# Attention of the experts: the input products of the recurrence are taken out of PSUM by ScalarE instead of VectorE

## The reference

```
h = _ln(relu(x @ ew1 + eb1) @ ew2 + eb2, eg, ebeta)
q, k, v = split(h @ aiw + aib)                       # 16 heads of 16
attn = softmax(einsum('bhqd,bhkd->bhqk', q, k) * SCALE)
h = einsum('bhqk,bhkd->bhqd', attn, v) @ aow + aob
# recurrence, forward and backward in time:
zg = xt @ Wi + h @ Wh + b                            # i, f, g, o gates, 4 x 256
```

## Time and profile before

| what | value |
|---|---|
| median of 3 runs | 6249.12 us (6246.4 to 6255.38) |
| the profiled execution, its own time | 6250.81 us |
| span of its trace | 6248.8 us |
| attention of the experts (all blocks) | about 790 to 2465 us |
| recurrence | about 2472 to 5860 us |
| mean granted TensorE clock | 0.964 of full speed |

### The profile page before, as it was taken

The page is one execution under the profiler, slowest core; times in us unless marked ns, Lnnn a source line. Parts: engine busy times, 40 slices in busy tenths (PEclk is TensorE's granted clock), DMA queues, the critical chain, the costliest instruction groups (busy, mean ns, idle before and its releaser), DMA issues. The chain is left out here.

```text
span 6248.8 us, 161662 instructions
## 1 busy us (share of the span) xinstructions
PE 5595.9 (90%) x59552; PEld 2263.0 (36%) x59552; DVE 4774.4 (76%) x14157; ACT 2351.6 (38%) x8487; POOL 1726.4 (28%) x8205
## 2 busy tenths in 40 slices
PE   7978788889899897999999999999999999998895
PEld 4545423233333232333333333333333333333443
DVE  4545676667576766999999999999999999994224
ACT  2334354355454444333333333333333333333332
POOL 0000000000000000555555555555555555552000
PEclk9989989999999998999999999999999999999997
DMA  0003443343432444011101110111101111012110
GB/s 12 0 24 129 127 80 78 95 73 74 94 74 64 93 89 139 19 34 20 34 14 34 20 34 24 24 34 20 34 14 34 33 21 34 14 20 69 35 68 10
DMA packets 378689, 303.02 MB, mean 48 GB/s; under 512 B 146073, under 2 KB 358681, under 8 KB 373562
## 3 DMA queue, kind: packets, MB, share of 16 engines
q1 hardware_dynamic: 378510, 301.15, 20.3%
HBM read 182.09 MB, written 120.59 MB: 48 GB/s over the span
## 5 line engine op out<-in xcount | busy, mean ns | idle before, releaser
L1300 PE MATMUL bank<-lparts,lstate 128*32 128x512 bf16 x49152 | 3006.1, 383 | 214.8 <-POOL lstate L1387 96.5
L1300 PEld LDWEIGHTS bank<-lparts,lstate 128*32 128x32 bf16 x49152 | 1133.0, 97 | 2088.2 <-POOL lstate L1387 1183.1
L1312 DVE STREAM_TRANSPOSE ltz<-bank 128x512 f32<-128x512 f32 x2048 | 1464.9, 715 | 129.8 <-PE bank L1300 51.4
L1357 ACT ACTIVATE lgate<-lz 128x48 f32<-128x48 f32 x2048 | 497.9, 243 | 2078.5 <-DVE lz L1318 2077.1
L1318 DVE TENSOR_REDUCE lz<-ltz 128x64 f32<-128x256 f32 x2048 | 1270.6, 620 | 0.0
L1051 DVE TENSOR_REDUCE bnegmax<-bank 128x1 f32<-128x512 f32 x1024 | 649.8, 680 | 251.2 <-PE bank L981 250.3
L1384 POOL TENSOR_TENSOR lstate<-lstate 128x16 f32<-128x16 f32 x2048 | 439.4, 215 | 1324.4 <-DVE lstate L1332 1250.4
L1270 POOL MEMSET lstate<- 128x256 f32 x1 | 0.3, 312 | 2471.4 <-POOLq L61 2471.4
L1096 ACT ACTIVATE wh<-bank 128x512 f32<-128x512 f32 x1024 | 554.4, 598 | 295.3 <-PE bank L1003 288.3
L1394 POOL COPY ltz<-wh 128x64 f32<-128x64 f32 x2048 | 593.6, 290 | 0.0
L883 PE MATMUL bank<-xT,bw 128*128 128x512 f32 x1024 | 537.0, 626 | 56.7 <-DVE bzs L894 51.7
(11 more groups left out here) (209 smaller groups left out, 4365.9 us busy)
## 6 DMA issues: line engine op xcount, KB each, us to landing
zx<-bzs SPq DMA_DIRECT2D x32, 2048.0 KB, 6.8
wh<-zx SPq DMA_DIRECT2D x64, 1024.0 KB, 8.7
bqp<-qk SPq DMA_DIRECT2D x198, 128.0 KB, 4.7
bkp<-qk SPq DMA_DIRECT2D x198, 128.0 KB, 7.9
qk<-eparts SPq DMA_DIRECT2D x96, 256.0 KB, 2.6
hs<-wh SPq DMA_DIRECT2D x32, 512.0 KB, 6.0
cmemT<-hs SPq DMA_DIRECT2D x32, 512.0 KB, 4.4
bw<-in_w_attend SPq DMA_DIRECT2D x4, 2304.0 KB, 11.4
```

Of the source, the lines that this page charges most:

```text
L1300: last = nc.tensor.matmul(bank[x][32 * q:32 * q + 32, :], top[:, x, k].rearrange("p m r -> p (m r)"), parts[:, way, g, k, n, q], start=k = ...
L1312: nc.vector.transpose(out, bank[x][:].rearrange("p (e n c) -> p e n c", e=2, n=8)).then_inc(turned[x], 1)
L1357: nc.scalar.activation(gate[:, x], z[:, x, :, 0:3], ACT.Sigmoid)
```

## The change

`keep_product` becomes a ScalarE instruction: an Identity activation with the bias column in place of VectorE's add. The operands, the output layout, the semaphores and the banks stay. It is called from ScalarE's stream: in a block with heads it stands in turn h behind the first exponential of head h - 2 and ahead of the other two; the last product is taken between the last two copies of the values. In the block with products alone all 16 takings stand behind ScalarE's `keep_projected`.

```diff
-        def keep_product(dve, n, banks, e, b):
+        def keep_product(act, n, banks, e, b):
 
             way, block = divmod(n, BLOCKS)
-            dve.wait_ge(z_mm, n + 1)
+            act.wait_ge(z_mm, n + 1)
             if block == 0:
-                dve.wait_ge(z_stored[way], 16 * (e * B + b) + 1)
-            nc.vector.tensor_scalar(zs[:, way, :, block], bank[banks[n % len(banks)]][:],
-                                    cols[:, COLS["lb"] + n:COLS["lb"] + n + 1], None, ALU.add).then_inc(z_kept, 1)
+                act.wait_ge(z_stored[way], 16 * (e * B + b) + 1)
+            nc.scalar.activation(zs[:, way, :, block], bank[banks[n % len(banks)]][:], ACT.Identity,
+                                 bias=cols[:, COLS["lb"] + n:COLS["lb"] + n + 1]).then_inc(z_kept, 1)
...
                     for h in range(NH + 2):
-                        if products and h >= 3:
-                            keep_product(dve, h - 3, BESIDE, e, b - 1)
                         if h < NH:
                             largest(h, 0)
...
-                    if products:
-                        keep_product(dve, NH - 1, BESIDE, e, b - 1)
...
                         if h >= 2:
-                            for kt in range(3):
-                                exponent(h - 2, kt)
+                            exponent(h - 2, 0)
+                        if products and h >= 3:
+                            keep_product(act, h - 3, BESIDE, e, b - 1)
+                        if h >= 2:
+                            exponent(h - 2, 1)
+                            exponent(h - 2, 2)
                         if 1 <= h <= NH:
                             keep_rows(h - 1)
                         if h >= 2:
                             exponent(h - 2, 3)
                     keep_values(2)
+                    if products:
+                        keep_product(act, NH - 1, BESIDE, e, b - 1)
                     keep_values(3)
...
                 def _(act):
                     keep_divided(act)
                     keep_projected(act)
+                    for n in range(NH):
+                        keep_product(act, n, ALONE, e, B - 1)
...
                     divide(dve)
-                    for n in range(NH):
-                        keep_product(dve, n, ALONE, e, B - 1)
```

## The result

The changed kernel takes 6427.56 us (median, 6425.46 to 6431.27), the kernel before 6250.51 beside it: a ratio of 1.0285, 95% interval 1.0272 to 1.0298. It is slower by 177 us. The forecast was 6417, in a range of 6340 to 6455.

What follows compares the result with a forecast made beforehand. TensorE sets the pace in the experts' attention, waiting for bank 7 to be emptied. Twelve blocks with heads cost 180 K - 26 = +168 us at K 1.08, other parts zero, giving 6417 us, range 6340 to 6455.

Steps and rivals of the forecast that it cites:

- The path of the head: Attention of the experts: product done, bank 7 emptied, next product, the rest; emptying bank 7 later lengthens the head by as much.
- The positions: Steady head, from first scores: first exponential at 0.85 us, taking at 1.34, next product's first half at 1.40 + K.
- K: Duration of one ScalarE taking of a product: forecast 1.08 us, between 0.687 (packed) and 1.142 (VectorE's).
- (a): Sign in the new profile: mean of the ScalarE instruction at L894 near 1.08 us; 0.69 means Rival 1.
- (b): Sign in the new profile: the steady head's period becomes 5.47 us + K.
- (c): Sign: waits at L883 now put down to ScalarE, TensorE idle about 1.4 us before each product's first half.
- (d): Sign: first exponential still 0.85 us after the head's first scores, the taking 0.49 behind it.
- (e): Sign: VectorE's work in the attention of the experts falls by 292 us with no gain.
- Rival 1: ScalarE pays nothing for spaced output: K 0.687 us, +98 us, 6347 us; chance 0.25.
- Rival 2: ScalarE as slow as VectorE, taking not overlapping the first exponential: +180 + 20 us, 6449 us; chance 0.13.
- Rival 3: Not slower: VectorE's relief wins, bank 7 empty once TensorE's third turned score is done; 85 us gained, 6164 us; chance 0.03.
- Rival 4: TensorE's clock falls to 1.2 GHz in the stretched heads: some 570 us more, near 6990 us; chance 0.02.

Runs made afterwards that it cites:

- the run ahead of E0: The changed kernel with ScalarE's taking of the product moved ahead of the first exponential of the turn, output still spaced: 6241.37 us, ratio 0.9984.
- the packed run ahead of E0: The changed kernel with the taking ahead of the first exponential and its 512 values written side by side (another product layout): 6156.10 us, ratio 0.9857.
- the packed run: The changed kernel, taking still behind the first exponential, its 512 values side by side instead of 32 bytes apart (another layout): 6348.95 us, ratio 1.0153.

## Why the prediction was right

*The path of the head* was read correctly. By the earlier trace rows TensorE waits for bank 7 and for nothing else, and the growth of that one wait, +184.1 us, is the growth of the stage, +183.8. Undoing only the place (6241) and only the spacing (6349) moved the time as the path says.

*The positions* came out as read from the kernel before: E0 at 0.85, the taking 0.49 behind it, P0 0.05 behind its end. The other classes of turns too, on the timeline of the changed kernel. Turn 3, whose P0 came at 1.84 before, and turn 16 against the earlier trace rows:

```profile
1107.22 0.59 PE L981 MATMUL bank<-bkp,bqp 96*128 96x512 bf16 x2
...
1109.79 1.13 PE L883 MATMUL bank<-xT,bw 128*128 128x512 f32 x2 [1.32 <-ACT bzs L894]
```

```profile
1073.81 0.81 PE L1003 MATMUL bank<-bqp,bkp 99*128 99x512 bf16 x3
1074.22 0.60 ACT L1092 ACTIVATE wh<-bank 128x512 f32<-128x512 f32 x1 [1.37 <-PE bank L1003]
1074.72 1.17 ACT L894 ACTIVATE bzs<-bank,bcols 128x512 f32<-128x512 f32 x1
1075.94 1.13 PE L883 MATMUL bank<-xT,bw 128*128 128x512 f32 x2 [1.32 <-ACT bzs L894]
```

P0 comes 2.57 after S0 (1.40 + 1.174 = 2.57), and 2.13 after T0 in turn 16 (0.97 + 1.174 = 2.14).

*K* is the term that was mis-sized: 1.08 forecast, 1.174 measured. ScalarE pays a surcharge of 0.487 us over its packed 0.687, where VectorE pays 0.391. 180 x 0.094 = 17 us, which makes 168 into 185; the stage grew by 183.8 and the median, against 6249.12, by 178.4. The upper end that the prediction gave for K, VectorE's 1.142, was 0.03 too low, yet the time it stood for (+180, 6429) still covered the measured 6428. So some 6 of the 17 us by which K was short did not show in the median: the other stages came out 3 us shorter, the stage 1.5 us under the sum, and the median 2 us lower against its profiled run than before. That the forecast missed by 11 us and not by 17 is chance.

*Why the whole of K appears in the sum*: because the taking now starts at 1.34, when VectorE's used to end. In a steady turn the change moves the start by 1.14 us, and that this is VectorE's K again is a coincidence of this kernel. Another order on ScalarE gives another sum, as the run ahead of E0 shows.

*The signs (a) to (e)*: (a) K is 0.09 above; (b) the steady turn is 5.47 + 1.17 = 6.64; (c) the wait is ScalarE's, with 1.32 us idle before P0 where about 1.4 was said, since T2's record ends at 1.24 and not at 1.07; TensorE does ask for bank 7 at about 1.07, as P0 at 1.09 in the packed run ahead of E0 shows; (d) as said; (e) VectorE's busy time is down by 269 us rather than 292, mostly since its takings had overlapped their neighbours' records, and without gain, which the load given back to it confirms.

*Costed at nothing*: later E1 and E2, and the blocks with products alone (their own run). For the exponentials, the turned scores T0 to T3 are what would wait, and their grouped lines before and in the changed kernel are:

```profile
L1003 PE MATMUL bank<-bqp,bkp 99*128 99x512 bf16 x1024 | 320.0, 392 | 1.4 <-ACT bqp L1088 0.9
L1003 PE MATMUL bank<-bqp,bkp 99*128 99x512 bf16 x1024 | 322.3, 394 | 1.4 <-ACT bqp L1084 0.9
```

TensorE's idle time ahead of them is 1.4 us in the whole stage both times, though E1 came at 2.29 instead of 1.34.

*The rivals.* Rival 1 (no surcharge) is refuted by K, and the packed run shows where it would have ended: 6349, as it said (6347). Rival 2 had the better K but a wrong lack of overlap: E0 is followed after 0.49, and the fourth exponential's late start in the earlier trace rows is something that belongs to the row copy. Rival 3 (relief wins) had the wrong mechanism for VectorE, but its condition, bank 7 empty before T2 ends, was brought about by two runs and gave 6156 and 6157 against its 6164. Rival 4 did not happen in the change and did one exponential further out, at 79 us of longer busy time instead of 570, since only a part of the matmuls ran at the lower level.

*Open*: whether spacing costs a surcharge on the engine's own pace or sets a pace of its own. The spaced totals are nearly one number on three engines, 1.174, 1.142 and 1.114 us, though the packed ones differ (0.687, 0.751). That reads like a pace of the writes, some 2.2 ns a value, rather than a surcharge to be added; it is a reading, no run shows it. Open too: what lets the clock fall in turns with a wait of 1.81 us and not in those with 1.32.

## What to carry to other kernels

When an eviction stands on the path of the engine that sets the pace, ask first when its input is ready and what the new engine does ahead of it: the input was ready at 0.20, E0 could not start before 0.85 and held the engine 0.49 more, and these 1.14 us in nearly every turn were the loss. Take the data out packed by whoever is free at that moment, release the bank, and leave the spaced write to an engine that nobody waits for. Price a strided write from the same stride on another engine, as a total and not only as a surcharge, and expect the step where only one value is left in 16 bytes.

## What the hardware showed that was not expected

- ScalarE writing 128x512 fp32 values out of PSUM with a bias column: 0.683 us packed, 0.709 at 8 bytes apart, 1.160 at 16, 1.174 at 32. GpSimd's copy from SBUF, without a bias, takes 1.114 at 32 bytes, no more than ScalarE and VectorE need out of PSUM.
- The clock of the whole stage went to 0.92 with a wait of 1.81 us in each turn, and stayed at 0.96 with one of 1.32. It cost 79 us of TensorE's time.
- A pair of fp32 matmuls has a record of 1.02 us where its weight load started 0.15 us ahead of it, and of 1.12 where both started together, behind a wait for the bank or behind the value products. That 0.1 us per turn is worth 17 us here, beyond the wait itself.
